# First attention: the softmax denominators from one product over 64 rounded sums and their 64 residues

## The reference, cut to what matters

```python
q = (query @ Wq + bq).reshape(B, L, NKV, G, HDIM)          # B = 8, L = 64, NKV = 8, G = 4, HDIM = 128
k_, v_ = jnp.split(kv @ Wkv + bkv, 2, axis=-1)              # kv: 8 x 1601 x 512
scores = jnp.einsum('blkgd,bmkd->bkglm', q, k) * scale
attn = jax.nn.softmax(scores, axis=-1)                      # over the 1601 context rows
o = jnp.einsum('bkglm,bmkd->blkgd', attn, v).reshape(B, L, NHEAD * HDIM)
return o @ Wo + bo
```

## Time and profile before

| | |
|---|---|
| median of three runs | 2604.69 us |
| the profiled execution | 2604.12 us |
| its span, first to last instruction | 2602.3 us |
| TensorE busy in the span | 2497.1 us, 96% |
| VectorE busy | 1726.8 us, 66% |
| ScalarE busy | 1489.4 us, 57% |
| GpSimd busy | 1348.7 us, 52% |
| the first attention's units, 64 of them | about 150 to 1883 us |

### The profile page before, as it was taken

The page is one execution under the profiler, slowest core; times in us unless marked ns, Lnnn a source line. Parts: engine busy times, 40 slices in busy tenths (PEclk is TensorE's granted clock), DMA queues, the critical chain, the costliest instruction groups (busy, mean ns, idle before and its releaser), DMA issues. The chain is left out here.

```text
span 2602.3 us, 42744 instructions
## 1 busy us (share of the span) xinstructions
PE 2497.1 (96%) x17160; PEld 2293.5 (88%) x17160; DVE 1726.8 (66%) x1956; ACT 1489.4 (57%) x2597; POOL 1348.7 (52%) x1009
## 2 busy tenths in 40 slices
PE   8999999999999999999999999999999599899878
PEld 6899999999999999999999999999987477654557
DVE  4157766777667776677766777667656699743473
ACT  3356655666556665566655666556543677523572
POOL 3335575485565558548556555854600599300352
PEclk9999999999999999999999999999999699999899
DMA  6520011111111101111111110100351300287200
GB/s 221 191 76 31 28 57 52 43 52 54 32 51 51 45 28 58 52 44 51 52 34 51 53 42 26 60 26 29 104 182 54 130 1 1 67 302 266 71 2 17
DMA packets 106989, 181.30 MB, mean 70 GB/s; under 512 B 8852, under 2 KB 72660, under 8 KB 105004
## 3 DMA queue, kind: packets, MB, share of 16 engines
q1 hardware_dynamic: 98476, 170.23, 19.7%
q10 hardware_dynamic: 8320, 8.39, 0.9%
HBM read 158.57 MB, written 20.02 MB: 69 GB/s over the span
## 5 line engine op out<-in xcount | busy, mean ns | idle before, releaser
L474 POOL TENSOR_TENSOR xa_pt_lo<-xs_st,xa_pt_hi 128x1024 fp32r<-128x1024 f32 x255 | 508.4, 2029 | 489.7 <-ACT xa_pt_hi L691 489.7
L54 PE MATMUL ctx_kv_ps<-ctx_wv_hi,ctx_hi 128*128 128x256 f32 x1536 | 431.8, 281 | 0.0
L56 PE MATMUL ctx_kv_ps<-ctx_wv_hi,ctx_lo 128*128 128x256 f32 x1536 | 430.2, 280 | 0.0
L55 PE MATMUL ctx_kv_ps<-ctx_wv_lo,ctx_hi 128*128 128x256 f32 x1536 | 430.2, 280 | 0.0
L54 PE MATMUL ctx_kv_ps<-ctx_hi,ctx_wk_hi 128*128 128x402 f32 (+1 forms) x1024 | 357.7, 349 | 2.4 <-DVE xa_k_lo L791 2.4
L55 PE MATMUL ctx_kv_ps<-ctx_lo,ctx_wk_hi 128*128 128x402 f32 (+1 forms) x1024 | 353.6, 345 | 0.0
L56 PE MATMUL ctx_kv_ps<-ctx_hi,ctx_wk_lo 128*128 128x402 f32 (+1 forms) x1024 | 352.5, 344 | 0.0
L798 DVE TENSOR_TENSOR xa_v_lo<-ctx_kv_ps,xa_v_hi 128x512 fp32r<-128x512 f32 x192 | 132.8, 692 | 244.0 <-ACT xa_v_hi L665 243.4
L55 PEld LDWEIGHTS ctx_kv_ps<-ctx_wv_lo,ctx_hi 128*128 128x128 f32 x1536 | 289.7, 189 | 0.0
L54 PEld LDWEIGHTS ctx_kv_ps<-ctx_wv_hi,ctx_hi 128*128 128x128 f32 x1536 | 288.6, 188 | 0.0
L56 PEld LDWEIGHTS ctx_kv_ps<-ctx_wv_hi,ctx_lo 128*128 128x128 f32 x1536 | 288.4, 188 | 0.0
(11 more groups left out here) (517 smaller groups left out, 6349.3 us busy)
## 6 DMA issues: line engine op xcount, KB each, us to landing
ctx_raw<-in_ctx_t SPq DMA_DIRECT2D x24, 804.0 KB, 6.5
ctx_wk_raw<-in_xa_wk SPq DMA_DIRECT2D x64, 256.0 KB, 2.8
ctx_wv_raw<-in_xa_wv SPq DMA_DIRECT2D x32, 512.0 KB, 4.3
n_back<-in_ctx SPq DMA_DIRECT2D x8, 1280.0 KB, 9.7
q_raw<-in_xa_wq SPq DMA_DIRECT2D x8, 1024.0 KB, 5.0
q_scratch<-q_q_sb ACTq DMA_DIRECT2D x8, 1024.0 KB, 4.5
ctx_q_raw<-q_scratch SPq DMA_DIRECT2D x64, 128.0 KB, 2.7
o_scratch<-xa_o_sb SPq DMA_DIRECT2D x64, 128.0 KB, 1.7
```

The costliest lines, as they stand in the source:

```text
L54: nc.tensor.matmul(out, left[0], right[0], start=first, stop=False)
L55: nc.tensor.matmul(out, left[0], right[1], start=False, stop=False)
L56: return nc.tensor.matmul(out, left[1], right[0], start=False, stop=last)
L474: nc.gpsimd.tensor_tensor(by_chunk(pt_lo, p), scored(j, p).rearrange("p g q c -> p g c q"), by_chunk(pt_hi, p).bitcast(F32), ALU.subtract) ...
```

## The change

ScalarE no longer rounds the sums. It copies their upper 64 partitions down to partitions 0 to 63 (`upper`, 64x256). VectorE adds the lower 64 to them (`folded_sums`, 64x256). GpSimd rounds the 64 folded sums into the lower half of `sum_halves` (a tensor_scalar, 64x256) and writes the residue into its upper half (64x256), each of the two followed by a wait for its own semaphore. One matmul of ones with the 128 partitions of `sum_halves` then takes the place of two. VectorE's add stands at three places: behind key tile 0 in even groups (for the unit before), behind value tile 3 in even groups (for the unit itself), and behind the sums in the last group.

```diff
             def sum_low(b, j):
-                pool.wait_ge(sum_hi_set, unit(b, j) + 1)
-                nc.gpsimd.tensor_tensor(sum_lo[:, :], sums[:, 1, :], sum_hi[:, :].bitcast(F32),
+                n = unit(b, j)
+                pool.wait_ge(fold_set, n + 1)
+                if n > 0:
+                    pool.wait_ge(o_full, n + 1)
+                nc.gpsimd.tensor_scalar(sum_halves[0:HP, :], folded_sums[:, :], 1.0, 1.0, ALU.mult,
+                                        ALU.mult).then_inc(sum_hi_set, 1)
+                pool.wait_ge(sum_hi_set, n + 1)
+                nc.gpsimd.tensor_tensor(sum_halves[HP:P, :], folded_sums[:, :], sum_halves[0:HP, :].bitcast(F32),
                                         ALU.subtract).then_inc(sum_lo_set, 1)
+                pool.wait_ge(sum_lo_set, n + 1)
...
             def denominators(b, j, alone=False):
                 pe.wait_ge(sum_lo_set, unit(b, j) + 1)
-                nc.tensor.matmul(d_ps(j, alone), ones_r[:, :], sum_hi[:, :], start=True, stop=False)
-                return nc.tensor.matmul(d_ps(j, alone), ones_r[:, :], sum_lo[:, :], start=False, stop=True)
+                return nc.tensor.matmul(d_ps(j, alone), ones_r[:, :], sum_halves[:, :], start=True, stop=True)
...
-            def sum_high(b, j):
-                n = unit(b, j)
-                act.wait_ge(sum_set, n + 1)
-                if n > 0:
-                    act.wait_ge(o_full, n + 1)
-                nc.scalar.activation(sum_hi[:, :], sums[:, 1, :], ACT.Copy).then_inc(sum_hi_set, 1)
+            def upper_sums(b, j):
+                act.wait_ge(sum_set, unit(b, j) + 1)
+                nc.scalar.activation(upper[:, :], sums[HP:P, 1, :], ACT.Copy).then_inc(upper_set, 1)
...
+            def folded(b, j):
+                dve.wait_ge(upper_set, unit(b, j) + 1)
+                nc.vector.tensor_tensor(folded_sums[:, :], sums[0:HP, 1, :], upper[:, :], ALU.add).then_inc(fold_set, 1)
...
                     maxima(b, j, 0)
                     key_tile(b, j + 1, 0)
+                    if not alone:
+                        folded(b, j - 1)
                     maxima(b, j, 1)
...
                     for g in range(2, NV):
                         value_tile(b, j, g)
+                        if g == 3:
+                            folded(b, j)
                     return
...
                     summed_in_two(b, j, 0)
                     summed_in_two(b, j, 1)
+                    folded(b, j)
                     normalise(b, j - 1)
```

More of the change, by code:

```diff
@@ L312, in cross_attention @@
         mx, sums = sc.sb("mx", [P, 2, NQ]), sc.sb("sums", [P, 2, NQ])
-        sum_hi, sum_lo = sc.sb("sum_hi", [P, NQ], F32R), sc.sb("sum_lo", [P, NQ], F32R)
+        HP = P // 2
+        upper, folded_sums = sc.sb("upper", [HP, NQ]), sc.sb("folded_sums", [HP, NQ])
+        sum_halves = sc.sb("sum_halves", [P, NQ], F32R)
         nmx = sc.sb("nmx", [P, NU])
@@ L335, in cross_attention @@
             sc.sem(n) for n in ("sub_set", "exp_set", "hi_set", "sum_part", "sum_set", "lo_set", "lo_dve"))
-        sum_hi_set, sum_lo_set = sc.sem("sum_hi_set"), sc.sem("sum_lo_set")
+        upper_set, fold_set, sum_hi_set, sum_lo_set = (sc.sem(n) for n in ("upper_set", "fold_set", "sum_hi_set", "sum_lo_set"))
         o_full, sum_full, rden_set, on_set, o_free = (
@@ L724, in first_unit @@
                 high(b, j, 3)
-                sum_high(b, j)
+                upper_sums(b, j)
                 for g in range(3, NV):
@@ L733, in group @@
                         high(b, j - 1, 0)
-                        sum_high(b, j - 1)
+                        upper_sums(b, j - 1)
                     key_tile(b, j + 1, 0)
```

## The result

The changed kernel takes 2637.27 us (median of 4 runs, 2636.76 to 2639.22), the kernel before 2604.95. The ratio is 1.0128, with a 95% interval of 1.0115 to 1.0140: 32.3 us slower, where 15.6 were forecast. The execution that was profiled took 2639.22 us, its span is 2637.4.

What follows compares the result with a forecast made beforehand. TensorE, busy for 96% of the span, was taken as the bound. From the profiled execution: 2604.12 - 7.4 (product) + 10.2 (VectorE's add) + 12.3 (context split) + 0.5 (last unit) = 2619.7 us, range 2607 to 2626.

Steps and rivals of the forecast that it cites:

- What bounds the kernel: In the stage holding nearly all units, TensorE has no idle time; matmuls removed win time, waits reaching it lose time.
- The removed product, 7.4 us: One 128x256 matmul fewer on TensorE in 63 units, at 0.118 us each: 7.4 us won.
- VectorE's add in even groups, 10.2 us: Add behind key tile 0 delays key tile 1's lo part, so TensorE's key tile 3 waits: 31 x 0.33 us lost.
- the maxima would still be in time: In even groups VectorE's maxima would end 0.33 us later, at 1017.22, still before TensorE's transposes at 1017.35: no second loss.
- GpSimd's late split, 12.3 us: In unit 6 of seven batches, the next context's split comes 4.00 us later, beyond its slack; TensorE waits: 12.3 us lost.
- all loads shift with the split: Loads of the next context start when buffers are split, so they come later too and GpSimd's waits recover nothing.
- rival (3): Context split recovers in GpSimd's waits for loads, so TensorE never waits for it: 2607.4 us; chance 0.09.
- GpSimd's step everywhere, no cost: GpSimd's added rounding makes its step 0.60 us longer per unit; in odd units 3.28 us of room absorbs it.
- rival (4): Residue written 64 partitions away takes GpSimd twice 0.74 us, making the split later still: 2624.9 us; chance 0.08.
- The last unit, 0.5 us: ScalarE, VectorE and GpSimd run one behind the other, so the residue TensorE awaits ends later: 0.5 us lost.
- (1): The gain alone: neither the add's wait nor the context split's reaches TensorE: 2596.7 us, faster; chance 0.08.
- (2): Only the context split's wait bites, VectorE's add in even groups costs TensorE nothing: 2609.5 us; chance 0.09.

Runs made afterwards that it cites:

- The product alone: Kernel before the change, with the residues' matmul left out and the residues still made: 2594.24 us, 0.9962 of the kernel before.
- the kernel with both moves: Changed kernel with the even groups' add put behind key tile 2 and the even unit's add behind value tile 2: 2595.42 us, 0.9967 of the kernel before.
- the earlier add alone: Changed kernel with only the even unit's own add moved, from behind value tile 3's lo part to behind value tile 2's: 2625.62 us.
- the PSUM operand: Changed kernel with ScalarE's copy of the upper sums put into PSUM, except in the last unit; add not moved: 2619.42 us.
- the later add alone: Changed kernel with only the even groups' add for the unit before moved, to behind key tile 2's lo part: 2609.25 us.

## Why the prediction was wrong, step by step

- **What bounds the kernel: right.** TensorE had no idle time, and each wait that reached it went into the time.
- **The removed product, 7.4 us: too small.** The product alone gave 10.0 us as a whole kernel. By the groups it is (54.30 - 54.01) / 2 = 0.145 us a unit, 9.0 us over 62 units. The distance of 0.118 us was right for the instruction; what else it slowed was not in the sum.
- **VectorE's add in even groups, 10.2 us: this step failed.** Its mechanism held: what the add puts into VectorE's order reaches TensorE with no slack to pay it from, 31 times. With one operand in PSUM the price was what the forecast said (54.35 - 54.02 = 0.33 us a group, 10.2 us). But the real add cost 54.93 - 54.02 = 0.91 us, 31 x 0.91 = 28.2 us; moving it away won 28.0. The row that was called the nearest, line 821, has the same 256 elements, but it reads one operand from PSUM; the add reads both from SBUF while GpSimd's lo part of the probabilities runs beside it. The bounds of that step, 0.27 to 0.47 us, were drawn around the wrong kind of row. The sentence that the maxima would still be in time fell with it: with the add at 0.40 us they are in time. The trace before had rows of the right kind, in a later stage. VectorE does the same add of 128x512 from SBUF twice, alone and beside a GpSimd instruction that reads SBUF:

```profile
2051.38 0.69 DVE L1747 TENSOR_TENSOR mamba_a_dt<-mamba_a_dt,mamba_w_work 128x512 f32<-128x512 f32 x1 [2.36 <-ACT mamba_a_dt L1786]
...
2052.16 1.64 POOL L1715 TENSOR_TENSOR mamba_a_dtu<-mamba_a_dt,mamba_u 128x512 f32<-128x512 f32 x1 [5.50 <-DVE mamba_a_dt L1747]
...
2052.59 1.76 DVE L1747 TENSOR_TENSOR mamba_a_dt<-mamba_a_dt,mamba_w_work 128x512 f32<-128x512 f32 x1
```

  It takes 0.69 us alone and 1.76 beside GpSimd, and ends 0.55 us behind the end of GpSimd's instruction (2053.80).
- **GpSimd's late split, 12.3 us: right in the place, the count and the size.** 4.16 us late where 4.00 was worked out, 7 waits, and 11.7 us by the run that undoes it alone. Most of the 0.16 is the wait of GpSimd for its own residue, 0.22 us of idle time where 0.08 was taken, so its step took 1.44 us and not 1.30. That all loads shift with the split was right for five batches; in batches 3 and 4 some 1.6 us of lateness were regained in the waits for loads, which is what rival (3) had, only too small to help.
- **GpSimd's step everywhere, no cost: right,** by the 54.02 us of the kernel with both moves. The residue written 64 partitions away took 0.73 us, no longer than in place: rival (4) falls.
- **The last unit, 0.5 us: too small.** From the last transposes to the next stage there are 22.72 us (1897.03 to 1919.75) against 20.53 (1865.12 to 1885.65), so 2.2. TensorE waits 2.27 us there instead of 1.39, so 0.9 more and not 0.5: the add stands beside a GpSimd piece here too and takes 0.73 us. Then the granted clock fell, which was not in the sum. The kernel with both moves has nearly the same wait, 2.29 us, without the fall, and loses 0.7 us there (21.26); the other 1.5 come with the fall.
- **The rivals.** (1), (2) and (3) all fall: both waits bit. None of them was that the add itself would be longer.
- **The sum again, with measured terms:** 2605.0 - 9.0 + 28.2 + 11.7 + 2.2 = 2638.1, against 2637.3 measured. The first two terms are from the distances of the groups, the third from the run with the earlier add alone, the fourth from the rows of the last unit.

The Trainium skill has the rule that was missed (SBUF — State Buffer, Who interferes with whom): a VectorE instruction with two SBUF inputs contends with a GpSimd instruction that reads SBUF, and the one that comes second waits until the first is done. The traces agree: the add ends 0.27 to 0.28 us behind the end of GpSimd's piece at either place, it takes 0.40 us with one operand in PSUM, and GpSimd's next piece takes 0.19 us longer in turn. The forecast did weigh another rule of the Trainium skill (VectorE: DVE Perf Modes, Two Vector instructions with no wait between them), which would have changed the price by 0.09 us, and priced nothing for the two engines together.

## What to carry to other kernels

An instruction is priced by a row of its own kind, and its kind includes where its operands lie and what the other engine does beside it: elements alone were wrong here by a factor of almost three. When work is to be added to an engine that looks idle, look for the place in its order where it waits for the bounding engine; the same add cost 28.2 us at one place and nothing a few instructions later, though it was longer there. A small gain on the bounding engine is worth having only when every step that makes it possible stands in such a gap: moving two calls turned 32.3 us slower than before into 8.8 us faster.

## What the runs showed of the hardware that was not expected

- A VectorE add of 64x256 with both operands in SBUF took 0.41, 0.98 or 1.42 us, with GpSimd idle or with 0.70 or 1.15 us left of GpSimd's instruction beside it; with one operand in PSUM it took 0.40 at the same place. GpSimd's next instruction lost about 0.2 us in the last two cases (2.65 against 2.46 us; 0.94 us for the piece of 65x256, which took 0.755 in the mean before).
- A wait of TensorE of 2.3 us was followed by the lower clock (1.2 GHz) for some 3 us in the changed kernel and in those with the PSUM operand and with the earlier add alone (0.60, 0.63 and 0.72 in the mean of the stretch), and by no fall at all in the kernel with both moves and in the one with the later add alone (1.00). What decides between the two is open.
- Taking out one matmul of 0.118 us from each unit won 0.145 us. Where the rest came from is open.
